# Softmax row sums by ACT, three transfers and a small reciprocal, and a new order of the stages, in a one-core language-model block

## The reference

```
h = table[x] + bias
xn = layernorm(layernorm(h)) * g + b
q, k, v = xn @ Wq, layernorm(h) @ Wk, layernorm(h) @ Wv      # 16 heads, 2 extra "null" keys and values each
q, k = l2norm(q) * q_scale, l2norm(k) * k_scale
p = exp(8 * q @ k.T + slope * distance, causal)
h = h + ((p @ v) / sum(p)) @ Wout
y = layernorm(h)
h = h + sum over the 2 best of 8 experts w_e * relu(y @ w1_e)^2 @ w2_e + relu(y @ cfc)^2 @ cproj
```

## Time and profile before

| | us |
|---|---|
| median of three executions | 3418.23 (3415.29 to 3420.38) |
| the profiled execution, its own time | 3428.19 |
| its span in the profile | 3425.9 |
| PE busy | 2829.8 (83%) |
| DVE busy | 2313.0 (68%) |
| POOL busy | 1460.9 (43%) |
| ACT busy | 1333.8 (39%) |
| mean granted TensorE clock | 0.913 of full |

### The profile page before, as it was taken

How to read it: one execution, slowest core, us unless ns; L and a number is a source line. 1 busy time by engine, 2 the same in 40 slices (tenths; PEclk the granted TensorE clock), 3 DMA queues, 4 the chain that set the end, 5 groups by cost and what they waited for, 6 DMA issues and landing times.

```text
span 3425.9 us, 47657 instructions
## 1 busy us (share of the span) xinstructions
PE 2829.8 (83%) x13729; PEld 1419.9 (41%) x13729; DVE 2313.0 (68%) x5792; ACT 1333.8 (39%) x2860; POOL 1460.9 (43%) x1765
## 2 busy tenths in 40 slices
PE   4788787888887877787888888888878788999999
PEld 3333333333333333333333333333333343666666
DVE  6767676768676878686767676767677776444443
ACT  3344434444444444444444343434344433111111
POOL 6354545444555454545454545454545453000000
PEclk8899998989898989898989898989999989999999
DMA  1000000000000000000000000000000010000000
GB/s 42 10 14 6 13 7 13 7 13 7 26 19 13 7 12 8 12 7 12 8 10 10 10 10 10 10 10 10 10 9 7 9 59 1 1 0 16 9 0 25
DMA packets 76232, 41.75 MB, mean 12 GB/s; under 512 B 19024, under 2 KB 74960, under 8 KB 75984
## 3 DMA queue, kind: packets, MB, share of 16 engines
q1 hardware_dynamic: 74448, 34.51, 3.8%
q0 software_dynamic: 1536, 4.20, 0.4%
HBM read 17.55 MB, written 4.19 MB: 6 GB/s over the span
## 4 chain that ended last, share of the span: by engine, by line
PE 39%; DVE 21%; POOL 19%; issue 17%; ACT 4%; POOLq 0%; DMA 0%; ACTq 0%; DVEq 0%
POOL acc L602 12%; PE ps L1188 7%; PE ps L1175 7%; DVE rl L897 5%; DVE ps L854 5%; PE ps L1056 5%; POOL rnorm L583 4%; PE ps L1127 4%; DVE tqk L827 4%; PE ps L1111 3%; DVE tqk L825 3%; PE ps L1084 3%; PE ps L1112 3%; PE ps L1053 2%; ACT probs L689 2%
## 5 line engine op out<-in xcount | busy, mean ns | idle before, releaser
L602 POOL TENSOR_TENSOR acc<-acc,probs 128x512 f32<-128x512 f32 (+4 forms) x944 | 897.0, 950 | 400.0 <-ACT probs L689 326.0
L689 ACT ACTIVATE probs<-ps,btab 128x512 f32<-128x512 f32 (+4 forms) x1408 | 761.9, 589 | 412.9 <-PE ps L1112 264.6
L1127 PE MATMUL ps<-probs,arena 128*64 128x512 f32 (+4 forms) x2816 | 652.4, 541 | 0.0
L854 DVE CUSTOM_DVE_ANT_0 ps<-ps,tab_l 128x512 f32<-128x512 f32 (+1 forms) x896 | 566.3, 672 | 101.4 <-PE ps L1084 98.9
L1111 PE MATMUL ps<-arena 128*128 128x512 f16 (+4 forms) x1408 | 504.4, 360 | 49.1 <-ACT probs L689 47.8
L1084 PE MATMUL ps<-arena 64*128 64x512 f16 (+4 forms) x1408 | 248.8, 346 | 306.4 <-DVE mx L854 300.6
L1112 PE MATMUL ps<-arena 128*128 128x512 f16 (+9 forms) x1408 | 495.8, 354 | 0.0
L580 POOL TENSOR_SCALAR nsq<-ssq 128x4 f32<-128x4 f32 (+1 forms) x272 | 74.6, 274 | 837.5 <-DVE ssq L814 836.8
L645 ACT ACTIVATE sq<-ps 128x256 f32<-128x256 f32 (+1 forms) x272 | 102.3, 376 | 733.2 <-PE ps L1056 731.2
L1056 PE MATMUL ps<-wqkv,xT 128*128 128x256 f32 (+1 forms) x1088 | 366.5, 471 | 0.0
L1084 PEld LDWEIGHTS ps<-arena 64*128 64x128 f16 x1408 | 74.9, 93 | 643.3 <-issue 640.0
(11 more groups left out here) (131 smaller groups left out, 3788.1 us busy)
## 6 DMA issues: line engine op xcount, KB each, us to landing
arena<-arena SPq DMA_DIRECT2D x512, 32.0 KB, 1.9
wqkv<-in_Wkv SPq DMA_DIRECT2D x32, 128.0 KB, 2.5
arena<-in_w SPq DMA_DIRECT2D x2, 2048.0 KB, 11.5
out<-h SPq DMA_DIRECT2D x8, 512.0 KB, 3.0
wqkv<-in_Wq SPq DMA_DIRECT2D x16, 128.0 KB, 2.4
arena<-augs SPq DMA_DIRECT2D x128, 1.0 KB
wo<-in_Wout SPq DMA_DIRECT2D x16, 128.0 KB, 2.2
h<-in_table,idx POOLq DMA_INDIRECT x32, 3.0
```

The lines of the kernel that those rows point to most:

```text
L602: pool.tensor_tensor(a, probs[0:rows, (n - 2) % PB, 0:GW] if first else a, p, ALU.add).then_inc(sum_pool, 1)
L689: nc.scalar.activation(probs[0:rows, n % PB, 0:w], bank(S0 + n % 2)[0:rows, 0:w], ACT.Exp, bias=btab[0:rows, hh, z:z + 1]).then_inc(exp_do ...
L854: nc.vector.tensor_tensor_reduce(bank(A0 + hd)[:, 0:w], bank(A0 + hd)[:, 0:w], tab, 1.0, NEG, ALU.add, ALU.max, mx[:, hd, it, c:c + 1]).th ...
L1127: mm(bank(O0 + o % 2)[DH * hd:DH * hd + DH, c0:GW], vt[t % 2][0:rows, jt, hd, :], probs[0:rows, n % PB, 0:GW - c0], start=(jt == 0), stop= ...
```

## The change

It has two parts.

**The reciprocal.** `sums` leaves its result in the shared bank as before. Now ACT copies the bank to `rl` (`keep_l`, 128x512), which also releases the bank. SP moves one row of each head to a column tile `l_col` of 128x8 (`turn_l`, two transfers). DVE takes the reciprocal of these 128x8 values in place (`inv_l`). SP writes them to a small tensor `l_row` in DRAM, waits until that has landed, and reads it back spread over all 64 partitions of each head (`spread_l`, two and two transfers). `divide` now waits for that and only multiplies.

```diff
+            def turn_l(t, ig):
+                o = NG * t + ig
+                sp.wait_ge(l_read, o + 1)
+                need(sp, li_out, 32 * o)
+                for hd in range(2):
+                    sp.dma_start(l_col[:, G * hd:G * hd + G], rl[DH * hd:DH * hd + 1, :]).then_inc(l_in, 16)
+            def spread_l(t, ig):
+                o = NG * t + ig
+                sp.wait_ge(li_ready, o + 1)
+                need(sp, rl_in, 32 * o)
+                for hd in range(2):
+                    sp.dma_start(l_row.ap()[hd, :].rearrange("(p k) -> p k", k=G), l_col[:, G * hd:G * hd + G]).then_inc(li_out, 16)
+                sp.wait_ge(li_out, 32 * (o + 1))
+                for hd in range(2):
+                    sp.dma_start(rl[DH * hd:DH * hd + DH, :], l_row.ap()[hd, :].partition_broadcast(DH)).then_inc(rl_in, 16)
+            def keep_l(t, ig):
+                o = NG * t + ig
+                act.wait_ge(l_ready, o + 1)
+                need(act, o_read, o)
+                nc.scalar.activation(rl[:, :], shared_of("sums", t, ig)[:, :], ACT.Copy).then_inc(l_read, 1)
+            def inv_l(t, ig):
+                o = NG * t + ig
+                dve.wait_ge(l_in, 32 * (o + 1))
+                nc.vector.reciprocal(l_col[:, :], l_col[:, :]).then_inc(li_ready, 1)
             def divide(t, ig):
                 o = NG * t + ig
-                dve.wait_ge(l_ready, o + 1)
-                nc.vector.reciprocal(rl[:, :], shared_of("sums", t, ig)[:, :]).then_inc(rl_ready, 1)
-                dve.wait_ge(rl_ready, o + 1)
+                dve.wait_ge(rl_in, 32 * (o + 1))
                 dve.wait_ge(pv_done, PAIR * t + 2 * last_block[ig] + 2)
```

**The order.** The plan's numbers change in every stage. The new `turn_of` moves each use of a shared bank until it is at least 0.9 units from all uses placed before it. Consumers are put further behind producers:

```diff
+    def turn_of(time):
+        apart = 0.65 if time < 0 else 0.9
+        for other in sorted(taken):
+            if abs(other - time) < apart - 1e-6:
+                time = other + apart
+        taken.append(time)
+        return time
+    LAGS = [dict(square=0.4, ssq=1.2, inv=1.9, unit=3.2, high=3.5, low=4.3, turn=4.8),
+            dict(square=0.9, ssq=2.0, inv=2.3, unit=4.2, high=5.0, low=5.8, turn=7.0)]
-            at(s0 + 1.2, "ssq", t, s)
-            at(s0 + 1.3, "inv_norm", t, s)
-            at(s0 + 2.6, "unit", t, s)
+            at(s0 + lag["ssq"], "ssq", t, s)
+            at(s0 + lag["inv"], "inv_norm", t, s)
+            at(s0 + lag["unit"], "unit", t, s)
...
-                at(s0 + 0.9, "shift", t, ig)
-                at(s0 + 1.7, "turn_shift", t, ig)
+                at(s0 + 1.1, "shift", t, ig)
+                s1 = turn_of(s0 + 5.5)
+                at(s1, "turn_shift", t, ig)
...
-            at(t0 + m - 0.9 * (m % 2) + 1.4, "sum_p", t, m)
-            at(t0 + (m | 1) + 1.9, "values", t, m)
+            at(t0 + m - 0.9 * (m % 2) + 1.85, "sum_p", t, m)
+            at(t0 + (m | 1) + 3.5, "values", t, m)
...
-            at(e0 + 2.6, "sums", t, ig)
-            at(e0 + 3.2, "divide", t, ig)
-                w0 = max(e0 + 5.3, wout_from[0] + 2)
+            s0 = turn_of(t0 + 2 * last_block[ig] + 1 + 4.4)
+            at(s0, "sums", t, ig)
+            at(s0 + 0.9, "keep_l", t, ig)
+            at(s0 + 0.9 + 0.1, "turn_l", t, ig)
+            at(s0 + 2.9, "inv_l", t, ig)
+            at(s0 + 2.9 + 0.1, "spread_l", t, ig)
+            at(s0 + 6.1, "divide", t, ig)
+                w0 = turn_of(max(sums_at[(t, ig)] + 7.7, wout_from[0] + 2.4))
```

More of the change, by code:

```diff
@@ L113, in project, with maxima @@
         for s in range(TK):
-            s0 = t0 + step * s
+            s0 = turn_of(max(t0 + step * s, s0 + 0.8 * step) if s else t0)
             at(s0, "proj", t, s)
-            at(s0 + 0.5, "square", t, s)
-            at(s0 + 1.2, "ssq", t, s)
-            at(s0 + 1.3, "inv_norm", t, s)
-            at(s0 + 2.6, "unit", t, s)
+            at(s0 + lag["square"], "square", t, s)
+            at(s0 + lag["ssq"], "ssq", t, s)
+            at(s0 + lag["inv"], "inv_norm", t, s)
+            at(s0 + lag["unit"], "unit", t, s)
             if s == 0:
-                at(s0 + 2.7, "null_v", t)
+                at(s0 + lag["unit"] + 0.1, "null_v", t)
             if s % 2 == 1 or s == T:
                 g = s // 2
[L124 to L130, removed]
+                at(s0 + lag["high"], "high", t, g)
+                at(s0 + lag["low"], "low", t, g)
+                s1 = turn_of(s0 + lag["turn"])
+                at(s1, "turn", t, g)
+                at(s1 + 0.8, "keep", t, g)
+                at(s1 + 0.8 + 0.1, "copy_low", t, g)
+                halves[(t, g)] = s1 + 3.0
+    def maxima(t, t0, step):
         s0 = t0 - step
         for n in range(UNITS):
-            s0 = max(s0 + step, halves((units[n][0] + 1) // 2) if halves else s0)
+            s0 = max(s0 + step, halves[(t, (units[n][0] + 1) // 2)])
             at(s0, "scores_a", t, n)
@@ L492, in _ @@
                     null_v(*which)
+                elif kind == "turn_l":
+                    turn_l(*which)
+                elif kind == "spread_l":
+                    spread_l(*which)
                 elif kind == "copy_low":
@@ L732, in _ @@
                     tables(*which)
+                elif kind == "keep_l":
+                    keep_l(*which)
                 elif kind == "store_x":
@@ L982, in _ @@
                     divide(*which)
+                elif kind == "inv_l":
+                    inv_l(*which)
                 elif kind == "ssq":
```

82 lines of the change are left out of this document (52 added, 30 removed).

## The result

The changed kernel takes 2950.4 us (median of four, 2945.7 to 2954.2) against 3419.3 us before: a ratio of 0.863, 95% interval 0.861 to 0.864. That is 469 us less, where 334 were forecast.

A forecast was written before the change was run, and what follows sets the result against it. No engine is full; PE, nearest, loses 32.1 us a step mostly waiting for a late DVE, plus low clock. Terms 6 + 6.5 + 3 + 7 - 1 = 21.5 us over 15.75 steps gave 3085 us, range 3020 to 3150 (wide 2965 to 3290).

The forecast's parts named there:

- (c): PE's other waits for maxima, 9.3 us a step, with DVE held by `unit` waiting on POOL: gain 3 us a step.
- (a): Long DVE reciprocal replaced by copy, transfers and small reciprocal: gain 6 of 11.85 us a step of PE's waits.
- (b): PE's wait at `turn_shift` for the shift, 7.3 us a step, now with more rows between: gain 6.5 us a step.
- (d): Granted clock over a step rises as PE's long pauses mostly go: gain 7 us a step, ends -2 and 14.
- (e): Added copies and SP issues, and later `sums` delaying POOL's adds: charge of 1 us a step, ends 0 and 4.
- The start: Kernel start, waiting for its first shift in both kernels: no change forecast.
- The end: Last group's sequence of 9.5 us stands bare where 3.4 did: 6 us lost.
- The signs: Right if `turn_shift` has no waits, `scores_a` waits under 10 us, clock 0.94 or more, step 145 to 160 us.
- the signs of being wrong: Wait before L983 of 4 us or more; L1195/L1196 waiting for `put_shift`; DVE over 85%; POOL's adds waiting long for `sums`.
- The transfers did not hold DVE: Rival: slow small-piece transfers, legs of 4.9 us, delay DVE at `divide` and the maxima; some 3525 us, chance 0.05.
- DVE did not become the bound: Rival: DVE can be loaded to no more than 75%, step 158 us, time about 3180 us, chance 0.17.
- Everything opens: Rival: PE's waits and the low clock both nearly go, 32 us a step gained, about 2920 us, chance 0.12.

The follow-up runs named there:

- both runs that separate it: New plan with the old whole-bank reciprocal, 3062.9 us; and the old plan with the new copy, transfers and small reciprocal, 3310.1 us.
- a free reciprocal: Changed kernel's new plan with the reciprocal of 8 of 512 columns straight from the bank, no transfers, most of the division left out: 2830.9 us.
- the projection's distances alone: Kernel before with the new distances inside a projection in the middle 14 of its 16 steps, all else old: 3217.0 us.
- the chain alone: Kernel before, its old plan kept, with the new reciprocal through ACT's copy, SP's transfers and DVE's 128x8 reciprocal: 3310.1 us, ratio 0.967.
- The order alone: Changed kernel's new plan of distances with the old reciprocal of the whole bank on DVE, no transfers: 3062.9 us, ratio 0.894.
- the faster versions: Changed kernel with `divide` and `wout` 1.5 units later and `ssq` 0.4 earlier: 2862.9 us; with `divide` and `wout` 2.5 later instead: 2851.5 us.

## Why the prediction was right and wrong

**The direction and the frame were right**: PE lost by waiting for a late DVE, and the low clock came with these pauses. The sum was too small, 21.5 us a step against 31.8. **The step that failed is term (c) and the terms beside it that were put at nothing.** The projection's distances stood at 3 us a step and carry 12.8; the spacing of the banks had no term and carries 6.5; the distances of the attend stage had none and carry 2.2. Each of these includes its share of the clock.

By the lines where PE waits, the whole execution divided by 15.75 steps reads: maxima 11.8 us a step less (300.6 to 114.5 in all) where (a) and (c) had 9 for them and `otf` together; `turn_shift` 7.3 less where (b) had 6.5; `scores` for `exp` 2.4 less (47.8 to 10.7) where nothing was forecast; `otf` 0.5 more. PE's busy time fell by 10.2 where (d) had 7.

**(a) The reciprocal: right.** I took 6 us a step, 95 us; both runs that separate it give 113, clock included. Under the new order part of that is the bank and not DVE's time: the 57.5 us that `proj` waits for the reciprocal's bank go with the chain, and the waits for maxima fall from 155.4 to 114.5 us. DVE's wait at the multiplication was put at 1.6 us a group; it is 102.3 us over 64 groups, 1.6. Its wait of 30.9 us at `inv_l` had no term. A group of the step before, one of the slower ones, on ACT, SP and DVE:

```profile
1425.19 0.60 ACT L767 ACTIVATE rl<-ps 128x512 f32<-128x512 f32 x1 [0.64 <-PE ps L1221]
...
1425.81 2.12 SPq L501 DMA_DIRECT2D l_col<-rl  x2
...
1429.41 0.20 DVE L976 RECIPROCAL l_col<-l_col 128x8 f32<-128x8 f32 x1 [0.17 <-DMA l_col<-rl]
...
1429.64 0.80 SPq L508 DMA_DIRECT2D l_row<-l_col  x2
...
1432.68 1.13 SPq L511 DMA_DIRECT2D rl<-l_row  x2
...
1436.38 0.69 DVE L983 TENSOR_TENSOR otf<-ps,rl 128x512 f32<-128x512 f32 x1 [3.62 <-DMA rl<-l_row]
```

Here it is 4.2 us from ACT's copy to `inv_l` (I said 3.2), and 7.0 from there to the multiplication (6.3). Over the groups in which DVE waits at the multiplication the median of the second is 6.3, as forecast. The three legs, from the first issue of a pair to the start of the next stage, have medians of 2.7 (where DVE waits for it), 2.4 and 3.6 us, against 2.5, 3.1 and 3.0 in the sum: near in total, and off by 0.7 and 0.6 at the last two, one too long and one too short. The Trainium skill's 2.0 us for a small transfer (DMA: Bandwidth & Descriptors, Anatomy of one DMA), which the page gives for transfers that GpSimd issues, would have been too little for each of the three, which hold two issues each; one store to `l_row` by itself lands in 1.5 us (median). So the 3.0 us that I read as agreement with DRAM being the slower target came with transfers of 512 KB; this store of 2 KB to DRAM lands sooner than the 1.9 us of 32 KB on the chip. That these waits reach PE in part is shown: `divide` 1.5 units later takes 86 us of them away and gains 54 to 64. 120 us lie between the changed kernel and a free reciprocal.

**(b) `turn_shift`: the number right, the cause not shown.** I read 7.3 us a step of waits at that line and credited 6.5 to its new distance. The waits went, but taking back most of that distance costs 4 us in all. In the step shown DVE came late to the shift: in the timeline of before it follows `unit` held by POOL (DVE idle 3.36 us until 1438.73, the shift at 1442.30, PE idle 5.51 us until 1443.63). The group of PE's waits shows this one at the line where it ended, not where it began. What ends it is not one edit: the projection's distances alone leave 82 us of the 96 for the shift, the chain alone 111, and the whole order with the transpose 2.4 instead of 6.1 units behind leaves 17.6. Whether a punctual DVE or the longer distance would do alone stays open.

**(c) The other waits for maxima: right in kind, far too small, the step that failed.** I took 3 us a step for DVE held by POOL's norms. The distances of a projection are worth 202 us, 12.8 a step, their share of the clock included, and 171 of these come from the 0.6 units between `inv_norm` and `unit`, when the rest is old; 74 when the rest is new. I had priced the wait DVE shows, 8.5 us a step, and not what it does: with `unit` early DVE waits 29 us more for norms, and PE 68 us more for maxima, at a line that has nothing to do with norms. The likely reason is that every later maximum in DVE's order is late by it; the order of the single instructions was not followed through. I also passed over the largest wait of the earlier trace rows, 20.0 us a step of `ssq` for ACT's squares. It cannot be all of the 202 us, since 50 us of it came with a gain and 139 us of it with a loss of 32 only; but no run takes it alone from the old distances. The old distances also bring back 40.5 us of waits for `exp`.

**(d) The clock: too small.** 7 us a step were forecast; PE's busy time in a step fell by 10.5, over the kernel by 160 us, of which 118 at `proj`.

**(e) and the spacing: missed.** I gave the distance of `values` nothing (it carries 35 us) and had no term at all for the spaced banks (102 us). Taken back one by one the four parts of the order make 202 + 102 + 35 + 4 = 343 of its 361 us. That the sum comes out so near does not mean that they never overlap: within the projection the same 0.6 units are worth 74 or 171 us, and the other numbers of the plan (`add_o`, the starts of projections and maxima, gates and experts) were not tried. POOL's wait for `sums`, charged at 1 us a step more, went from 17.6 to 72.8 us in all, 3.5 a step more; whether it is on the path is open.

**The start: missed.** Forecast nothing, it lost 29 us. The order alone, without the chain, already starts its first multiplication at 149.0, so it accounts for 20 of them. Which number of the plan does it was not tried. The end, put at 6 us lost, gained 5.

**The signs.** Right were `turn_shift`, the maxima (4.8 us a step) and the clock (0.967); the step of 143.3 us lies just outside 145 to 160. Of the signs of being wrong DVE stayed under 85%, but three showed: 2 of the 47 waits before L983 are over 4 us (the longest 5.6), L1195 waits 8.0 us in all for `put_shift`, and POOL waits 72.8 us in all for `sums`.

**The rivals.** The transfers did not hold DVE enough to matter for the sign: the leg with pieces of 16 bytes took 2.7 us, not 4.9. DVE did not become the bound at 78% in the step (111.8 of 142.6). "Everything opens", 2920 us at 0.12, was the nearest, and the faster versions, down to 2852, show that even that was not the end. What stays open: how the spacing of the banks makes its 102 us beyond the 30 at `wout`, how the 0.6 units before `unit` come to be worth so much, and why `ssq` closer to `square` is 16 us faster.

## What to carry to other kernels

A wait belongs to the engine that began to be late, not to the line where the last engine stood: before crediting a wait to a moved instruction, follow the releaser back until it waits itself. In kernels whose engines run fixed orders, the distance of a consumer behind a slow helper engine (here 0.6 of a unit, about 1 us) was worth 74 us by itself and 171 with the distances ahead of it old. That is of the size of what moving a 3.4 us instruction off the busy engine brought (113 us). A chain of three transfers costs its consumer nothing only if about as much time lies between as the chain takes (here 11.4 us from the copy to the multiplication, median of the groups that waited); put the consumer there and measure once more a unit later. And taking an edit back tests only what the run really takes back: here a second rule of the plan had moved the stage again.

## What the hardware showed that was not expected

Taking a row of one partition apart into 128 pieces of 16 bytes held SP no longer than a `copy_low` of 64 partitions by 256 columns. The medians of one issue are 594 and 592 ns (the 2.12 us for two in the rows above are an outlier; 52 of the 64 pairs took 1.15 to 1.18 us):

```profile
L501 SPq DMA_DIRECT2D l_col<-rl x128: 495/594/1605, 145.9 to 2407.1; - x128
L526 SPq DMA_DIRECT2D arena<-arena x256: 461/592/1314, 68.9 to 2288.9; - x128
```

The issues that write `l_row` took 358 ns and those that spread it 496. A reciprocal of 128x8 takes 195 ns, one of 128x512 3357: 6.3 ns for each further column between these two. And a lower clock is a third of what waits cost here: 317 us fewer waits came with 160 us less busy time for the same 13729 matmuls. Over the runs the clock rises almost without exception as PE idles less, from 0.913 at 596 us idle to 0.982 at 201 us.
